# Values in column halves in two attentions; in the first one six stack buffers, transfers issued by GpSimd, and the maxima split ahead of the additions

## What is computed

```python
for s in (0, 2):                                  # plain, and rolled by 2
    xs = jnp.roll(x, (-s, -s), axis=(1, 2)) if s > 0 else x
    for idx, (nh, hs, nw, ws) in enumerate([(1, 32, 8, 4), (8, 4, 1, 32)]):
        ...                                       # 64 channels, 8 windows of 128 positions, 8 heads of width 8
        attn = softmax(einsum('whqc,whkc->whqk', qw, kw))
        ow = einsum('whqk,whkc->whqc', attn, vw) + lw
```

```python
attn = softmax(einsum('bhqd,bhkd->bhqk', q, k))
out = einsum('bhqk,bhkd->bhqd', attn, v)
```

## Time and profile before

| | us |
|---|---|
| Time, median of 3 runs (3897.05 to 3911.96) | 3906.41 |
| Time of the profiled execution | 3902.64 |
| its span, first to last instruction | 3900.8 |
| mean granted TensorE clock, share of full speed | 0.92 |
| TensorE matmul busy | 3362.7 (86%) |
| VectorE busy | 2734.7 (70%) |
| ScalarE busy | 2099.7 (54%) |
| GpSimd busy | 1000.6 (26%) |

### The profile page before, as it was taken

One profiled execution on the slowest core, in us unless ns is written; L12 is line 12 of the kernel. 1 busy time (PEld: TensorE's weight loads), 2 busy tenths in 40 slices (PEclk: granted clock), 3 DMA queues, 4 the chain that ended last, 5 costly groups with the idle time before them and its releaser, 6 DMA issues. The chain is left out here.

```text
span 3900.8 us, 68078 instructions
## 1 busy us (share of the span) xinstructions
PE 3362.7 (86%) x24815; PEld 1499.4 (38%) x24815; DVE 2734.7 (70%) x4437; ACT 2099.7 (54%) x2668; POOL 1000.6 (26%) x868
## 2 busy tenths in 40 slices
PE   6997778846779999999999999778987949999999
PEld 4664445523522222222222222163356734444444
DVE  3227767646479999999899999443449647777776
ACT  1224667711217777777777777633432325555555
POOL 0001343320000000000000000004420048888887
PEclk9997877868869999999999999979999859999999
DMA  4443555510320000000000100004410114323230
GB/s 149 129 130 85 114 119 117 106 20 0 118 79 16 21 18 25 16 22 21 21 22 16 27 16 16 11 11 151 151 48 0 45 46 114 100 81 101 89 93 27
DMA packets 137471, 243.06 MB, mean 62 GB/s; under 512 B 36776, under 2 KB 49232, under 8 KB 136720
## 3 DMA queue, kind: packets, MB, share of 16 engines
q1 hardware_dynamic: 137232, 239.79, 22.6%
HBM read 167.36 MB, written 56.62 MB: 57 GB/s over the span
## 5 line engine op out<-in xcount | busy, mean ns | idle before, releaser
L1075 DVE TENSOR_REDUCE mxv<-mx_ps 128x1 f32<-128x512 f32 x2048 | 1277.0, 683 | 90.1 <-PE mx_ps L934 71.9
L1050 ACT ACTIVATE PT<-st_ps 128x1024 f32<-128x1024 f32 x1024 | 997.1, 1022 | 297.5 <-PE st_ps L947 297.3
L934 PE MATMUL mx_ps<-KS,QS 24*128 24x512 f16 x2048 | 613.7, 394 | 113.8 <-DVE mxv L1075 96.4
L2024 POOL TENSOR_TENSOR hg<-u,gb 128x512 f32<-128x512 f32 x352 | 580.3, 1654 | 131.5 <-DVE u L1985 101.2
L961 PE MATMUL o_ps<-PT,VA 128*32 128x512 f32 x4096 | 550.9, 610 | 0.5 <-ACT PT L1050 0.5
L947 PE MATMUL st_ps<-QS,KS 26*128 26x512 f16 x2048 | 400.6, 388 | 9.2 <-ACT TX L1040 8.4
L669 DVE TENSOR_REDUCE mxv<-mx_ps 128x4 f32<-128x512 f32 x512 | 319.8, 684 | 122.4 <-PE mx_ps L544 118.1
L1985 DVE TENSOR_TENSOR u<-h_ps,s 128x512 f32<-128x512 f32 x352 | 243.1, 691 | 190.7 <-ACT s L1946 185.6
L1946 ACT ACTIVATE s<-h_ps 128x512 f32<-128x512 f32 x352 | 210.0, 596 | 284.0 <-PE h_ps L1901 284.0
L947 PEld LDWEIGHTS st_ps<-QS,KS 26*128 26x128 f16 x2048 | 96.5, 91 | 559.2 <-issue 481.6
L365 POOL TENSOR_TENSOR mt<-nm,less 128x16 f32<-128x16 f32 x64 | 13.8, 216 | 1113.9 <-DVE nm L1080 1113.9
(11 more groups left out here) (237 smaller groups left out, 4747.2 us busy)
## 6 DMA issues: line engine op xcount, KB each, us to landing
gb<-g SPq DMA_DIRECT2D x64, 512.0 KB, 3.7
gb<-g SPq DMA_DIRECT2D x32, 1024.0 KB, 5.6
QK<-qk SPq DMA_DIRECT2D x128, 192.0 KB
qk<-hl SPq DMA_DIRECT2D x80, 256.0 KB, 3.3
RB<-d SPq DMA_DIRECT2D x48, 256.0 KB, 3.5
gb<-g SPq DMA_DIRECT2D x64, 192.0 KB, 5.7
qk<-hl SPq DMA_DIRECT2D x64, 128.0 KB, 3.2
v<-vs SPq DMA_DIRECT2D x32, 256.0 KB
```

The source lines that it names most:

```text
L934: nc.tensor.matmul(mx_ps[:, use % 3, :], rows(QS, g // 2, j, STACK)[:, t * C:(t + 1) * C], rows(KS, g // 2, j, STACK)[:, half * HALF:(half ...
L1050: nc.scalar.activation(PT[:, n % 2, 2 * a:2 * a + 2], st_ps[:, a], ACT.Exp, scale=1.0 / SHIFT ** 2).then_inc(st_free[a], 1)
L1075: nc.vector.tensor_reduce(mxv[:, g % 2, j, t, half:half + 1], mx_ps[:, slot], AX.X, ALU.max).then_inc(mx_free, 1)
L2024: nc.gpsimd.tensor_tensor(hg[:, n % HG_SLOTS], u[:, n % H_SLOTS], gb[:, s, tile], ALU.mult).then_inc(gated, 1)
```

## The change

In both attentions `values` is cut into two halves by columns (in the first attention by windows, which are column blocks of 128). The half comes right behind each pair of `max_scores`, the turn after the first half, and `fill_array` moves ahead of the scores of a = 0. In the first attention, besides: six stack buffers, with `load_qk` for five units ahead, issued after `load_rows`; three `OR` and four `ON` buffers; half of `regroup` before the rows and half after the stacks; `load_v`, the store of the inverses and the broadcasts issued by GpSimd; `split_max` ahead of `finish`; and the memset of the keys by stack, as float32 with the bits of two float16.

```diff
+MAX_UNITS = 2.0 ** 113 * (1 + 30720 / 2.0 ** 23)
...
+    STACKS, OUTS, HALVES = 6, 3, 4
...
+    def stack(i, u):
+        return group(i, u) % STACKS          # group(i, u) = i * U + u
...
                 def image(i, kind):
                     for u in range(U):
                         if i or u:
                             sp.wait_ge(st_ready[1], i * STEPS + 4 * u)
-                        if u == 0 and kind != "first":
-                            load_qk(i, 3)
-                        if u and kind != "last":
-                            load_qk(i + 1, u - 1)
+                        prior = (i - (u == 0), (u + 3) % U)
+                        if group(i, u):
+                            load_den(*prior)
+                            regroup(*prior, (0, 1))
                         if kind != "last" or u < 3:
                             sp.wait_ge(mx_free, i * PER + (LEAD + MX[kind]["turn", u, TURNS[u][-1]] + 1 + 3))
-                            load_rows((u + 1) % 4)
-                        if u:
-                            load_den(i, u - 1)
-                            regroup(i, u - 1)
-                        elif kind != "first":
-                            load_den(i - 1, 3)
-                            regroup(i - 1, 3)
-                        if kind != "last" or u < 1:
-                            sp.wait_ge(va_done, i * U + (u + 2))
-                            load_v(i + (u + 3) // 4, (u + 3) % 4)
-                        if u == 3:
-                            spread(i, 0)
-                        if u == 1 and kind != "first":
-                            spread(i - 1, 1)
+                            load_rows(i + (u == 3), (u + 1) % U)
+                        if group(i, u) + 5 < B * U:
+                            load_qk(i + (u + 5) // U, (u + 5) % U)
+                        if group(i, u):
+                            regroup(*prior, (2, 3))
...
-                    if a == 1:
+                    if a == 0:
                         fill_array(nc, st_ps[:, a, 1], ident, KS[:, k, s, 0:HALF])
...
-                    for w in range(4):
+                    for w in (2 * half, 2 * half + 1):
                         for j in range(4):
...
-                    mm.then_inc(pv_done, 1)
+                    if half:
+                        mm.then_inc(pv_done, 1)
...
                             scores(i, n, a)
                             for j in pair:
                                 ahead(j)
+                            if n:
+                                values(i, n - 1, a)
+                            elif kind != "first":
+                                values(i - 1, STEPS - 1, a)
                             if a:
                                 continue
...
-                        if n:
-                            values(i, n - 1)
...
-                nc.vector.memset(KS, MAX_UNIT).then_inc(ones_set, 1)
+                for k in range(STACKS):
+                    nc.vector.memset(KS[:, k].rearrange("p s n -> p (s n)").bitcast(F32), MAX_UNITS).then_inc(ones_set, 1)
...
             def _(pool):
+                def load_v(i, u):
+                    pool.dma_start(VS[:, u % 2], v_scr[i, u]).then_inc(v_loaded[u % 2], 16)
+                def store_inverse(i, h):
+                    pool.wait_ge(inverted, i * 2 + (h + 2))
+                    pool.dma_start(d_scr[i, h].rearrange("a p n -> p a n"), RD[:]).then_inc(rd_stored, 16)
+                def spread(i, h):
+                    pool.wait_ge(rd_stored, 16 * (i * 2 + h + 1))
+                    if i:
+                        pool.wait_ge(x_done, i * 2 + h - 1)
+                    for part in range(2):
+                        src = d_scr[i, h, part].rearrange("(s a) n -> s (a n)", s=8)
+                        pool.dma_start(RB[64 * part:64 * part + 64, h],
+                                       src.unsqueeze(0).to_broadcast([D] + list(src.shape))).then_inc(rb_loaded[h], 16)
...
                             expand_v(u + 1)
-                        if u % 2 == 0 and kind != "first":
-                            finish(i - 1, u // 2)
+                        if kind != "last" or u < 1:
+                            pool.wait_ge(va_done, i * U + (u + 2))
+                            load_v(i + (u + 3) // 4, (u + 3) % 4)
+                        if u == 1 and kind != "first":
+                            store_inverse(i - 1, 1)
+                        if u == 3:
+                            store_inverse(i, 0)
                         if kind != "last" or u < 2:
                             split_max(u, i * PER + (LEAD + MX[kind][4 * u + 3, 1] + 1 + 3), i * 12 + (3 * u + 6))
+                        if u == 1 and kind != "first":
+                            spread(i - 1, 1)
+                        if u == 3:
+                            spread(i, 0)
+                        if u == 0 and kind != "first":
+                            finish(i - 1, 0)
+                        if u == 2 and kind != "first":
+                            finish(i - 1, 1)
...
# token_attention
+                    at = slice(2 * C * half, 2 * C * (half + 1))
                     for j in range(4):
-                        mm = nc.tensor.matmul(o_ps[32 * j:32 * j + 32, :], VA[:, g // 2 % 2, kt, j, :], PT[:, n % 2, j, :],
-                                              start=(kt == 0), stop=(kt == KT - 1))
+                        mm = nc.tensor.matmul(o_ps[32 * j:32 * j + 32, at], VA[:, g // 2 % 2, kt, j, :], PT[:, n % 2, j, at],
+                                              start=(kt == 0 and half == 0), stop=(kt == KT - 1 and half == 1))
```

More of the change, by code:

```diff
@@ L410, in mx_uses, with group @@
         return numbered(uses)
+    def group(i, u):
+        return i * U + u
+    def stack(i, u):
+        return group(i, u) % STACKS
     MX = {kind: mx_uses(kind) for kind in ("first", "mid", "last")}
@@ L468, in load_den @@
                     sp.wait_ge(o_free, i * STEPS + (4 * u + 5))
[L469 to L475, removed]
+                    o = group(i, u) % OUTS
+                    sp.dma_start(DEN[:, u // 2, u % 2], OR[D:C:32, o].rearrange("j s n -> j (s n)")).then_inc(den_loaded[u], 16)
@@ L598, in image @@
                             if with_max:
-                                pe.wait_ge(qk_loaded[(u + 2) % 4], i * 64 + (64 if u < 2 else 128))
+                                g = group(i, u + 2)
+                                pe.wait_ge(qk_loaded[g % STACKS], 64 * (g // STACKS + 1))
                         def ahead(j):
@@ L620, in image @@
                                     turn(use)
-                        if n:
-                            values(i, n - 1)
-                        elif kind != "first":
-                            values(i - 1, STEPS - 1)
                 periods(pe, image)
-                values(LAST, STEPS - 1)
+                for half in range(2):
+                    values(LAST, STEPS - 1, half)
             @block.scalar
@@ L634, in take @@
                     act.wait_ge(pv_done, i * STEPS + (n + 3))
[L635 to L638 removed]
+                    g = group(i, u)
+                    if n % 4 == 0 and g >= OUTS:
+                        before = g - OUTS
+                        act.wait_ge(regrouped[before % U], 128 * (before // U + 1))
+                        act.wait_ge(den_loaded[before % U], 16 * (before // U + 1))
+                    nc.scalar.copy(OR[:, g % OUTS, n // 2 % 2, n % 2 * HALF:(n % 2 + 1) * HALF], o_ps[:]).then_inc(o_free, 1)
                 def image(i, kind):
@@ L1011, in image @@
                                 ahead(j)
+                            if n:
+                                values(i, n - 1, kind, a)
+                            elif kind != "first":
+                                values(i - 1, STEPS - 1, "mid", a)
                             if a:
@@ L1018, in image @@
                                 turn(use)
-                        if n:
-                            values(i, n - 1, kind)
-                        elif kind != "first":
-                            values(i - 1, STEPS - 1, "mid")
                 periods(pe, image)
-                values(LAST, STEPS - 1, "mid")
+                for half in range(2):
+                    values(LAST, STEPS - 1, "mid", half)
                 project(LAST, st_per(0) - 1)
```

148 lines of the change are left out of this document (72 added, 76 removed).

## The result

The changed kernel takes 3784.49 us (median of 4 runs, 3779.51 to 3795.13) against 3906.4; the ratio is 0.969, with a 95% interval of 0.967 to 0.972. That is 122 us or 3.1% faster; forecast were 3748 us, 158 less than the median, with a range of 3708 to 3818. The profiled execution took 3781.18 us, its span is 3779.4, 121.4 less than before.

The account below looks back on a forecast made before the run. Prediction: late maxima rows bound the first attention, the TensorE-VectorE loop through three maxima buffers the second. 3902.6 - 85 (first) - 66 (second) - 4.6 (start) + 1 (end) = 3748 us; own range 3715 to 3785, whole range 3708 to 3818.

Parts of the forecast that it names:

- signs named for being right: First attention: no row waits over 2 us, clock about 0.95 or more, groups near 11.4; second: steps 2.42, groups near 19.8.
- signs of being wrong: TensorE waiting for the split; rows landing over 3 us after issue; reductions 2.53 apart, VectorE never idle; second-attention clock below 0.9.
- the 85 us of the first attention: First attention, main stretch: 30.75 groups at 11.4 us, 350.6 against 435.8 us; 36 to 101 us less.
- the order that the prediction blamed for the late rows: First attention, SP's queue: four stack loads (768 KB) issued ahead of the maxima rows; TensorE's 13 waits total 58.4 us.
- VectorE would not be faster when fed: Rival, second attention: reductions beside exponentials take 0.63 us, not 0.60, so steps stay 2.53; 3814 us, chance 0.13.
- Second attention, the turn: Second attention, each group of eight steps: turn shrinks from 0.64 to 0.45 us, 12 us over 62 groups.
- First attention, loop and halves: First attention: loop through the one output buffer takes 2.70 us a step, 11.1 a group; halves bring nothing.
- First attention, mean group: First attention: 11.1 us a group plus 0.3 for the broadcasts gives 11.4, bounds 10.9 to 13.
- That just fits: First attention: rows issued at about 7.7 us land 10.4 to 10.8 into the group, needed by 10.8.
- GpSimd as the bound: Rival, first attention: GpSimd held until transfers land, or broadcasts delaying rows by 2 us; 3797 to 3806 us, chance 0.17.
- Start and end: First attention: smaller memsets save 4.6 us at the start (0 to 6); last store and broadcasts cost 1 us (0 to 3).
- the slower rival: Second attention: small waits between halves drop the clock, steps some 3.6 us; 4409 us if all 496, chance 0.04.

## Why the prediction was right, and where its terms were off

The time lies in the forecast range, though the median is only half a microsecond inside the forecast's own (3715 to 3785), and what sets the step in each stage was right. Of the signs named for being right only the steps of 2.42 in the second attention came as said. The others did not: the waits for the rows are up to 2.3 us, two of them over 2; the clock in the first attention is 0.90 and not 0.95; the groups take 11.79 and 20.10 and not 11.4 and 19.8. Of the signs of being wrong one came about: rows that land over 3 us after their issue. And that the 85 us of the first attention came out at 73 is in part luck: the order that the prediction blamed for the late rows costs nothing by itself in the changed kernel, while the regrouping buffers, to which it gave no price, are worth 52 us in the new order.

- **Second attention, steps: right.** 2.42 forecast and measured, half of the values 0.57 (0.55), VectorE's own time is the bound. That VectorE would not be faster when fed, a rival, did not come about. What the prediction passed over in half a sentence, the fill "moves in there", was over two fifths of the gain: with the fill at its old place a step is 2.49.
- **Second attention, the turn: mis-sized.** Forecast was 0.45 a group, on the ground that the maxima are ready when VectorE wants them. Measured is 0.74, more than the 0.64 before; 62 x 0.29 = 18 us are the whole miss in this stage (66 against 48.5). Half the values, the fill and the scores stand between the turn's last maxima and the next. Moving one fill took the turn to 19.78 - 19.36 = 0.42.
- **First attention, loop and halves: right in mechanism.** Step 2.66 for 2.70, clean group 10.80 for 11.1, shown by the 0.32 that a misplaced fill adds to each step. That the halves bring nothing was a little low: 6 us by the clean groups.
- **First attention, mean group: mis-sized.** 11.79 for 11.4, 12 of the 85 us. In the group shown, the issue of the rows ended 8.1 us after the fill that begins their group (402.89 to 410.96; forecast 7.7), and TensorE went on 4.4 us after that, where the prediction had 2.7 to 3.1. (The times in the earlier trace rows count from the start of an issue, from where it was 5.6; the prediction added them to its end, and so counted the 1.2 us of issue twice.) "That just fits" did not fit there; the 0.3 us for the broadcasts stood for a wait of up to 2.3 and the cold steps behind it. But the landing is not the whole of the 12 us: the rows issued first, which takes these waits away, gave back 2 to 9. TensorE's waits that are most likely for its instructions, 5.5 us in the changed kernel, were no term of the sum.
- **First attention, cause of the late rows: wrong in part.** The prediction blamed the four stack loads ahead of the rows and the order on SP. Undoing that order in the changed kernel costs no time that can be told. The queue was late from what it did before: with the store, its landing and the broadcasts on SP the main stretch is 32 us longer. In the new order it also waits for GpSimd's additions, unless there are four regrouping buffers (414.3 against 362.7 us). The prediction gave these buffers no price. Undone one at a time, the five parts tried cost 6 (stacks), 32 (issues), 52 (buffers), 6 (additions) and 11 us (halves), together more than the 73 gained: they depend on each other, and which share each has in the late rows of the kernel before is not shown.
- **GpSimd as the bound: no.** Its issues took 0.6 to 0.8 us, less than the 1.0 taken, and it waited for VectorE ahead of 29 of 30 splits. The lateness that did come was the other half of that rival, broadcasts delaying rows, at about a quarter of its price (0.39 us a group over the forecast, against 1.6).
- **Start and end.** -6.3 for -4.6, +1.2 for +1. The 6.6 us at the stage's end, GpSimd's DRAIN, are a term that was missing.
- **The clock** of the second attention's steps stayed at 1.00, so the slower rival did not come about.

The misses add up: 11.9 + 17.5 + 6.6 - 1.7 + 0.2 = 34.5 us, less the 1.3 of the other stages 33.2, by which the profiled execution (3781.2) lies over 3748.

## What to carry to other kernels

Ask of a late transfer what its queue was waiting for, not only what stands ahead of it: issues that filled idle time of the queue were free here, while one wait for a landing or for another engine's result held everything behind it. Where an engine is fed through a few buffers, place each filler (fills, halves, turns) by the gap between two feedings; a move of 0.32 us of work that computes nothing was worth 17 us of the first attention and 20 of the second. Count the buffers that a reordering needs as a part of it, since here the new order without two of them loses 50 us.

## What was not expected of the hardware

- With transfers issued by GpSimd in the stage, its DRAIN at the end of the stage takes 6.60 us, to the hundredth the same in all eleven such kernels, and 0.03 in the three in which only SP issued. 7.71 us pass between the last work of the stage and the first of the next, against 1.11 to 1.13.
- TensorE's waits with no cause in the profile's views end 2.6 to 3.0 us after a 16 KB packet of an instruction queue began: twelve over 0.25 us, 14.2 us in all, in the main stretch of the run with the rows first.
- Landing times were longer where the traffic was: the 256 KB of the values took a median of 3.1 us at 105 GB/s, 5.3 at 116 in the run in which SP issued them again, and 6.1 at 124 when GpSimd did; the 64 KB store 2.7, 3.8 and 5.6. From the second to the third the issuing engine changes too, and no run separates it from the traffic.
- A VectorE that shows no idle time can still be kept waiting: 0.623 against 0.61 us a reduction, because every fourth starts 0.69 and not 0.62 us after the one before, by the place of one matmul.
